# Query tables that read the queries by grid column from a copy made by GpSimd

## The chip, the cores and the metric

The kernel runs on one core of one Trainium2 chip. The metric is the device time of one execution in microseconds (us), from three runs. One further execution was recorded by the hardware profiler; all durations below come from it. The engines are PE (TensorE, with its weight loads shown apart as PEld), DVE (VectorE), ACT (ScalarE), POOL (GpSimd) and SP (which only issues DMAs here).

## The reference

The program is a small audio tower: a token mixer with a linear attention, an expert layer that adds the two best of eight experts, an attention with relative positions in two directions, and a second expert layer with one expert per token. Only the third part matters here. There are B = 4 batches of N = L = 750 tokens, and 12 heads of 64.

```python
def rel_pos_embed(N, table_v, table_h):
    n = N - 1
    s = int(n ** 0.5)                       # 27
    r = jnp.arange(n)
    dv = r[None, :] // s - r[:, None] // s
    dh = r[None, :] % s - r[:, None] % s
    iv = jnp.clip(dv, -L, L) + L + 1        # L = 14
    ih = jnp.clip(dh, -L, L) + L + 1
    iv = jnp.pad(iv, ((1, 0), (1, 0)))
    ih = jnp.pad(ih, ((1, 0), (1, 0)))
    return table_v[iv] + table_h[ih]
...
attn = jnp.einsum('bhid,bhjd->bhij', q, k) * scale
rpk = rel_pos_embed(N, rk_v, rk_h)
attn = attn + jnp.einsum('bhid,ijd->bhij', q, rpk) * scale
attn = jax.nn.softmax(attn, axis=-1)
out = jnp.einsum('bhij,bhjd->bhid', attn, v)
rpv = rel_pos_embed(N, rv_v, rv_h)
out = out + jnp.einsum('bhij,ijd->bhid', attn, rpv)
return out.transpose(0, 2, 1, 3).reshape(B, N, H * HD) @ wproj + bproj
```

All tokens but one stand on a grid of 27 columns: 749 = 27 * 27 + 20, so the grid has 28 rows, of which the last has only 20 tokens. A query's product with the relative embedding depends only on the query's own row (or column) and the key's row (or column). So for each grid row g, the queries of that row are multiplied by one small table, and for each grid column by another.

## The kernel before, in words

**Halves.** The attention goes through 8 halves: 4 batches by 2 groups of 6 heads (HG = 6, held as NPR = 3 pairs of heads, two heads on 128 partitions). A half has a long stretch of 36 steps (`words`: scores, exponentials, products with the values, at about 3 us a step) and ends in a boundary, where the work of two halves meets: `value_tables` finishes the old half, `query_tables` prepares the new one, and `boundary` projects the old output and begins the new maxima. A loop runs over the first 3 batches; the fourth is written out after it. The first half's `query_tables` stands ahead of the loop, so 7 of the 8 lie in a boundary between two halves.

**What holds the queries.** `pairs` is a tile of 128 partitions by 3 by 750 in float32. ACT fills it (L2382) from PE's products of the new half, six pieces of 375 tokens. The last pieces come just after the old half's last step.

**The query tables (L2118 to L2145).** PE makes seven sets of products into four PSUM banks (the `t_banks`, two in tile a_S and two in a_M): sets 0 to 2 are the grid rows (table `rqv`), sets 3 to 5 the grid columns (table `rqh`), set 6 token 749 alone. A matmul of a row reads 27 tokens that lie side by side in each of the three pairs (81 numbers a partition). A matmul of a column reads every 27th token (`pairs[:, :, g:g + GRID * (n - 1) + 1:GRID]`, L1980), 28 or 27 of them in each pair (84 or 81 numbers), 108 bytes apart. A float32 matmul has two records in the trace, and two tables are worked at a time, in the left and the right 64 columns of the array. Sets 0 and 1 have 24 matmuls together, set 2 has 4, sets 3, 4 and 5 have 12, 8 and 7.

**Who empties the banks.** `relative_rows` copies every set to `work`, ACT the even heads (L2427), DVE the odd heads (L2726), both in the order of the sets. Since there are four banks, PE may begin set m only when both have copied set m - 4, and the products of the values (`token_values`, L2176) wait for the fifth and sixth set. When all seven sets are out on both sides, ACT rounds the queries (`qhi`, L2438), and only then can the maxima begin (L2150).

**DVE's order at a boundary** is written by hand: parts of the keys (L2632), the reciprocal of the sums (L2654), the additions of the column part of the values (L2666, paced by PE's L2112), three multiplications by the reciprocals (L2671; these come back through DRAM, issued by SP at L1898), then its part of `relative_rows` (L2726), then the projection's additions and the maxima.

**GpSimd** does one thing in this stage: `qlo`, the rest of the rounded queries, six subtractions of 127x750 a half (L1970). It idles through the boundary until ACT has written `qhi`.

Of the kernel before, what the change touches and what calls it, by code (L numbers as in the profile page):

```python
# [12 lines left out]
F32 = mybir.dt.float32  # L13
# [3 lines left out]
ALU = mybir.AluOpType  # L17
# [3 lines left out]
B, D, L = 4, 64, 750  # L21
KS = (3, 5, 7)
E = len(KS) * D
CH, P = 6, 125
# [729 lines left out]
RING = 4  # L754
# [47 lines left out]
def moe(nc, keep, A, h, ident, cfg, out, st=None, w1=None, wr=None, row=None, room=None, share=None, Y=None,  # L802
# [4 lines left out]
    with ctx:  # L807
# [3 lines left out]
        def sem(n):  # L811
            return keep.enter_context(nc.semaphore(f"{name}_{n}"))
# [9 lines left out]
        n = sb("n", [P, NT, E]) if cfg.gated else None  # L822
# [7 lines left out]
        if not cfg.gated:  # L830
            n = xn
# [18 lines left out]
        if not known:  # L850
            st = sb("st", [P, NT, 6])
# [68 lines left out]
        psY = ctx.enter_context(nc.psum_tensor(f"{name}_psY", [128, 512], F32))  # L920


        s_w, s_r, s_z, s_X, s_cst = sem("w"), sem("r"), sem("z"), sem("X"), sem("cst")

        s_v, s_ln, s_sd, s_n = sem("v"), sem("ln"), sem("sd"), sem("n")
# [8 lines left out]
        s_lt, s_lc = sem("lt"), sem("lc")  # L934
        s_col, s_turn = sem("col"), sem("turn")

        s_in = [sem(f"in{j}") for j in range(RING)]
        s_st = [sem(f"st{j}") for j in range(RING)]

# [782 lines left out]
class Room:  # L1722
# [5 lines left out]
    def __init__(self, nc, sb):  # L1728


        wq, wkv = sb("wq", [128, 4, HG * HD], F32R), sb("wkv", [128, 4, HG * HD], F32R)
        wp = sb("wp", [128, NPR, E])
        rqv, rqh = sb("rqv", [128, NVG + 1, 64]), sb("rqh", [128, GRID + 1, 64])
        rv = sb("rv", [128, NVG + 1, 64])
        bp = sb("bp", [P, E])
        qhi, qlo = sb("qhi", [128, HG, L], F32R), sb("qlo", [128, QLO, L], F32R)
        khi, klo = sb("khi", [128, HG, L], F32R), sb("klo", [128, HG, L], F32R)
        work = sb("work", [128, HG, LW])
        pairs = sb("pairs", [128, NPR, L])
        outs = sb("outs", [128, NPR, LW])  # L1740

        turning = sb("turning", [128, GRID * NVG])

        vhi, vlo = sb("vhi", [P, CH, HG, 128], F32R), sb("vlo", [P, CH, HG, HD], F32R)


        hn = sb("hn", [128, 3, L + 2], F32R)

        PT = sb("PT", [P, 2, 2 * HP])
        Phi, Plo = sb("Phi", [P, 2, 2 * HP], F32R), sb("Plo", [P, 2, 2 * HP], F32R)  # L1750

# [12 lines left out]
        later = [vhi[:].rearrange("p c h d -> p (c h d)").bitcast(F32), vlo[:].rearrange("p c h d -> p (c h d)").bitcast(F32)]  # L1764

        def tokens(x, lo):
            return x[:, lo * CH * E:(lo + 1) * CH * E].rearrange("p (c e) -> p c e", e=E)

        self.got = [[tokens(flat[k], 0) for k in range(2)]] + [[tokens(later[0], 2 * b + k) for k in range(2)]
                                                               for b in range(2)] + [[tokens(later[1], k) for k in range(2)]]  # L1770
        self.all = (wq, wkv, wp, rqv, rqh, rv, bp, qhi, qlo, khi, klo, work, pairs, outs, turning, vhi, vlo, hn, PT, Phi, Plo, nb, rdb, dcol, oh, ohT, st, rstd, mv_, mean, nmx, mrow)


def window_attention(nc, keep, A, h, ident, W4, room, share, Y0, s_back, mv1, rstd1, w11, X1):

    ctx = ExitStack()
    with ctx:
        def sem(n):
            return keep.enter_context(nc.semaphore(f"a1_{n}"))

        (wq, wkv, wp, rqv, rqh, rv, bp, qhi, qlo, khi, klo, work, pairs, outs, turning, vhi, vlo, hn, PT, Phi, Plo, nb, rdb, dcol, oh, ohT, st, rstd, mv_, mean, nmx, mrow) = room.all
        psS = [ctx.enter_context(nc.psum_tensor(f"a1_S{i}", [128, 2, 512], F32)) for i in range(2)]
        psM = ctx.enter_context(nc.psum_tensor("a1_M", [128, 2, 512], F32))
        psO = ctx.enter_context(nc.psum_tensor("a1_O", [128, 2, 512], F32))

        s_bpw = sem("bpw")
        s_bp = sem("bp")
        s_wkv, s_wq, s_wp = sem("wkv"), sem("wq"), sem("wp")  # L1790
        s_w, s_oh, s_oz, s_og = sem("w"), sem("oh"), sem("oz"), sem("og")
# [18 lines left out]
            "table_product": 2 * NTS,  # L1810
            "table_rows_act": 2 * NTS,
            "table_rows_dve": 2 * NTS,
            "qhi_ready": 12,
            "qlo_ready": 12,
            "row_scores": 72,
# [132 lines left out]
        @block.gpsimd  # L1948
        def _(pool):

            for u in range(HG):
                pool.memset(klo[64:128, u].bitcast(F32), 0.0)
            for u in range(QLO):
                pool.memset(qlo[64:128, u].bitcast(F32), 0.0)
            pool.memset(work[0:64, :, L:LW], 0.0)
            pool.memset(turning[64:128], 0.0)
            for u in range(HG):
                last = pool.memset(work[64:128, u], 0.0)
            last.then_inc(s_oz, 1)
            pool.wait_ge(s_oz, 1)  # L1960
            keep.clear_old(pool)
            with pool.Fori(0, B) as i:
                wait = waiter(pool, i)
                for half in range(2):
                    for u in range(half * HG, half * HG + HG):

                        wait("qhi_ready", u + 1)
                        if u % HG >= QLO:
                            wait("scores_ready", (u - QLO + 1) * CH)
                        pool.tensor_tensor(qlo[0:ONE, u % HG % QLO, :], work[0:ONE, u % HG, 0:L],  # L1970
                                           qhi[0:ONE, u % HG, :].bitcast(F32), ALU.subtract
                                           ).then_inc(sg["qlo_ready"], 1)

        def query_tokens(side, g, n):

            if side == "v":
                return pairs[:, :, GRID * g:GRID * g + n]
            return pairs[:, :, g:g + GRID * (n - 1) + 1:GRID]

        def group_tokens(view, side, g, n):  # L1980
# [34 lines left out]
        def _(pe):  # L2015
# [99 lines left out]
                                start=True, stop=True)  # L2115
                    last.then_inc(sg["rel_product"], 1)

            def query_tables(i, half):  # L2118

                wait = waiter(pe, i)  # L2120
                wait("pairs_ready", half * 6 + 6)
# [9 lines left out]
                for m, (side, runs) in enumerate(TABLE_SETS):  # L2131
                    bank_free(m)
                    table = rqv if side == "v" else rqh
                    for a in range(max(len(gs) for gs, n in runs)):
                        for z, (gs, n) in enumerate(runs):
                            if a < len(gs):
                                last = nc.tensor.matmul(
                                    t_banks[m % 4][64 * z:64 * z + 64, a * NPR * n:(a + 1) * NPR * n],
                                    table[:, gs[a] + 1, :], query_tokens(side, gs[a], n), start=True, stop=True)
                    last.then_inc(sg["table_product"], 1)  # L2140
                m = NTS - 1
                bank_free(m)
# [195 lines left out]
            keys_part(0, 0, 5)  # L2338
            pe.wait_ge(s_w, 16 * 3)
            pe.wait_ge(s_oz, 1)  # L2340
            query_tables(0, 0)
            boundary(None, (0, 0))

            pe.wait_ge(s_og, 1)
# [606 lines left out]
```

## Time and profile before

| | |
|---|---|
| three runs, median | 1724.31 us |
| lowest and highest | 1723.38 and 1725.91 us |
| profiled execution, first to last instruction | 1721.1 us |
| PE busy | 1534.4 us (89%), 10815 records |
| DVE busy | 1190.8 us (69%) |
| ACT busy | 988.4 us (57%) |
| POOL busy | 341.2 us (20%), 79.1 us of it `qlo` |
| mean granted TensorE clock | 0.947 of full speed |

The profile gives the execution's span, and no time of its own beyond that; the span stands 3.2 us under the median of the runs. The attention stage runs from about 400 to 1510 us. PE is busy nearly all of it, but a busy PE isn't PE at its peak, and at each boundary it waits several times. What an edit is worth there is read from which engine comes last at each wait, not from these shares. The granted clock of PE has two levels, 1.00 (2.4 GHz) and 0.50 (1.2 GHz).

### The profile page before, as it was taken

Reading aid. Unit: us, or ns where it says so; the run is one execution under the profiler, and the core shown is the slowest. Engines: PE = TensorE matmul, PEld = TensorE weight load, DVE = VectorE, ACT = ScalarE, POOL = GpSimd, SP = SyncE. Lnnn points to the kernel's source line nnn. Section 1 sums busy time; section 2 is a strip of 40 time slices with the busy share of each in tenths; the row PEclk is TensorE's granted clock in tenths of the full one; section 3 lists DMA queues with packets and bytes.
Section 4 is the critical chain, followed back from the end, with each engine's and each line's share of the span. In section 5 each row is a group of like instructions: output and inputs, shape, how many; then the busy total and the mean of one; then the engine's idle time right before and its main releaser. Section 6 shows DMA issues by size and latency. Waiting matters only on the chain. (4 is left out here: it accounts for less than half of the span.)

```text
span 1721.1 us, 32129 instructions
## 1 busy us (share of the span) xinstructions
PE 1534.4 (89%) x10815; PEld 1409.8 (82%) x10816; DVE 1190.8 (69%) x2245; ACT 988.4 (57%) x1777; POOL 341.2 (20%) x499
## 2 busy tenths in 40 slices
PE   5983999937999999899999999999999999848997
PEld 5762999936898898899898899998989889737996
DVE  4887555549775786786787677678677678575443
ACT  5541222226677578578677667667757757562221
POOL 5131566640000000110100010000000010014443
PEclk9985999968999999999999999999999999958999
DMA  8212111164101101100110110110010111091221
GB/s 266 70 51 80 48 57 57 56 142 120 44 11 38 45 11 39 46 11 19 30 44 11 31 45 20 30 44 20 29 45 10 39 35 51 20 291 49 63 58 29
DMA packets 61936, 94.83 MB, mean 55 GB/s; under 512 B 15644, under 2 KB 46511, under 8 KB 61422
## 3 DMA queue, kind: packets, MB, share of 16 engines
q1 hardware_dynamic: 52606, 72.92, 14.7%
q0 software_dynamic: 9200, 20.21, 4.1%
q8 instruction: 78, 1.28, 0.3%
q14 instruction: 52, 0.43, 0.1%
HBM read 72.58 MB, written 21.06 MB: 54 GB/s over the span
## 5 line engine op out<-in xcount | busy, mean ns | idle before, releaser
L2678 DVE TENSOR_REDUCE a_nmx<-a_M 125x1 f32<-125x752 f32 x256 | 240.7, 940 | 129.7 <-PE a_M L2150 128.8
L2500 ACT ACTIVATE a_Phi<-a_S 125x756 fp32r<-125x756 f32 x288 | 231.0, 802 | 156.2 <-PE a_O L2273 146.5
L2803 DVE TENSOR_TENSOR a_Plo<-a_PT,a_Phi 125x756 fp32r<-125x756 f32 x288 | 280.9, 975 | 52.5 <-ACT a_PT L2500 51.7
L1970 POOL TENSOR_TENSOR a_qlo<-a_work,a_qhi 127x750 fp32r<-127x750 f32 x48 | 79.1, 1656 | 996.0 <-PE a_S L2254 509.3
L2500 ACT ACTIVATE a_PT<-a_S 125x756 f32<-125x756 f32 x288 | 230.0, 799 | 0.0
L2254 PE MATMUL a_S<-a_qhi,a_khi 128*125 128x378 f32 x576 | 155.4, 351 | 12.9 <-issue 6.1
L2266 PE MATMUL a_O<-a_Phi,a_vhi 125*128 125x378 f32 x576 | 150.3, 342 | 1.3 <-ACT a_PT L2500 1.3
L2273 PE MATMUL a_O<-a_Plo,a_vhi 125*128 125x378 f32 x576 | 147.5, 337 | 1.0 <-DVE a_Plo L2803 0.9
L2254 PE MATMUL a_S<-a_qhi,a_klo 128*125 128x378 f32 x576 | 146.9, 336 | 0.0
L2254 PE MATMUL a_S<-a_qlo,a_khi 128*125 128x378 f32 x576 | 146.9, 336 | 0.0
L2269 PE MATMUL a_O<-a_Phi,a_vlo 125*64 125x378 f32 x576 | 146.4, 336 | 0.0
L2150 PE MATMUL a_M<-a_khi,a_qhi 127*125 127x376 f32 x512 | 132.2, 339 | 0.4 <-DVE a_nmx L2678 0.4
L1215 PE MATMUL m_psY<-m_w,m_hidT 128*128 x696 | 130.0, 331 | 2.7 <-DVE m_hidT L1572 2.7
L1215 PEld LDWEIGHTS m_psY<-m_w,m_hidT 128*128 128x128 f32 x696 | 114.4, 190 | 9.5 <-issue 9.5
L2254 PEld LDWEIGHTS a_S<-a_qhi,a_khi 128*125 128x125 f32 x576 | 98.3, 187 | 26.4 <-issue 13.5
L2273 PEld LDWEIGHTS a_O<-a_Plo,a_vhi 125*128 125x128 f32 x576 | 104.1, 189 | 14.4 <-DVE a_Plo L2803 4.3
L1299 ACT ACTIVATE m_xT<-m_psX 128x128 fp32r<-128x128 f32 x85 | 23.6, 277 | 155.8 <-PE m_psX L1139 155.8
L1151 PE MATMUL m_psG<-m_w,m_xT 128*128 x540 | 110.9, 352 | 0.5 <-issue 0.4
L2266 PEld LDWEIGHTS a_O<-a_Phi,a_vhi 125*128 125x128 f32 x576 | 102.0, 190 | 11.1 <-issue 8.1
L2254 PEld LDWEIGHTS a_S<-a_qhi,a_klo 128*125 128x125 f32 x576 | 103.9, 187 | 0.0
L2254 PEld LDWEIGHTS a_S<-a_qlo,a_khi 128*125 128x125 f32 x576 | 103.8, 187 | 0.0
L1151 PEld LDWEIGHTS m_psG<-m_w,m_xT 128*128 128x128 f32 x540 | 93.7, 190 | 5.4 <-issue 3.2
(440 smaller groups left out, 3050.3 us busy)
## 6 DMA issues: line engine op xcount, KB each, us to landing
a_qhi<-a_rdens SPq DMA_DIRECT2D x48, 187.5 KB, 3.4
a_wkv<-a_w4k SPq DMA_DIRECT2D x8, 768.0 KB, 5.1
a_wq<-a_w4q SPq DMA_DIRECT2D x8, 768.0 KB, 6.6
a_wkv<-a_w4v SPq DMA_DIRECT2D x8, 768.0 KB, 5.6
m_w<-in_m_w SPq DMA_DIRECT2D x8, 576.0 KB, 9.3
m_X<-m_xn SPq DMA_DIRECT2D x8, 504.0 KB
m_w<-in_m_w SPq DMA_DIRECT2D x8, 384.0 KB, 6.2
m_w_ahead<-in_m_w SPq DMA_DIRECT2D x8, 384.0 KB, 8.1
```

The source lines that it names most:

```text
L1151: last = nc.tensor.matmul(psG[buf][:, g, 0:half], tokens, w1[0:rows_, bass.ds(e, 1), k, g * half:(g + 1) * half].rearrange("d o f -> d (o ...
L1215: last = nc.tensor.matmul(psY[:, 0:E], hidT[:, k * 128:(k + 1) * 128], w2[:, bass.ds(here, 1), k, :].rearrange("f o e -> f (o e)"), start= ...
L1299: nc.scalar.activation(xT[:, buf, 0, :], psX[:, 0:SLOT], ACT.Copy)
L1970: pool.tensor_tensor(qlo[0:ONE, u % HG % QLO, :], work[0:ONE, u % HG, 0:L], qhi[0:ONE, u % HG, :].bitcast(F32), ALU.subtract).then_inc(sg[ ...
L2150: last = nc.tensor.matmul(bank[0:P, a, 0:376], qhi[0:ONE, u % HG, c * P:(c + 1) * P], khi[0:ONE, u % HG, a * 374:a * 374 + 376], start=Tru ...
L2254: last = nc.tensor.matmul(psS[wd % 2][0:P, a, 0:HP], kk[:, u % HG, at], qq[:, PART[a]:PART[a] + HP], start=(x == 0), stop=(x == 2))
L2266: nc.tensor.matmul(psO[:, a, 0:HP], vhi[:, c, u % HG, :], Phi[:, wd % 2, at[a]], start=(c == 0), stop=False)
L2269: nc.tensor.matmul(psO[0:HD, a, 0:HP], vlo[:, c, u % HG, :], Phi[:, wd % 2, at[a]], start=False, stop=False)
L2273: last = nc.tensor.matmul(psO[:, a, 0:HP], vhi[:, c, u % HG, :], Plo[:, wd % 2, at[a]], start=False, stop=(c == CH - 1))
L2500: last = nc.scalar.activation(to[:, wd % 2, :].rearrange("p (a l) -> p a l", a=2), psS[wd % 2][0:P, :, 0:HP], ACT.Exp, scale=SCALE)
L2678: v.tensor_reduce(nmx[:, u % 2, c:c + 1], bank[0:P, :, 0:376], AX.XY, ALU.max, negate=True).then_inc(sg["max_ready"], 1)
L2803: v.tensor_tensor(Plo[:, wd % 2, :], PT[:, wd % 2, :], Phi[:, wd % 2, :].bitcast(F32), ALU.subtract).then_inc(sg["exp_rest"], 1)
```

## The change

GpSimd gets a second job at each of the 7 boundaries between halves. When the old half's last product with the values is done and the new half's queries are all in `pairs`, it copies `pairs` into a new tile `by_column` (128 partitions by 3 by 750), sorted by grid column: 20 columns of 28 tokens, then 7 columns of 27. That takes 9 copies, 3 a pair of heads. The tile lies over the memory of `PT` and the first part of `Phi`, which the old half's last steps have just finished reading, and which the new half writes only after its query tables. Sets 3 to 5 of `query_tables` then read 28 or 27 tokens side by side, and the first matmul of set 3 waits for GpSimd's last copy. The query tables of the very first half read as before. A semaphore `turning` is added that nothing waits for, and a few semaphores of the expert layers are created in another order.

```diff
+        with ExitStack() as early:
+            by_column = early.enter_context(nc.sbuf_tensor("a1_by_column", [128, NPR, L], F32))
         PT = sb("PT", [P, 2, 2 * HP])
...
+            def turn_pairs(i, half):
+
+                wait = waiter(pool, i)
+                wait("values_added", (half + 1) * HG * CH)
+                if half == 0:
+                    wait("pairs_ready", 12)
+                else:
+                    waiter(pool, i + 1)("pairs_ready", 6)
+                pool.sem_inc(s_turning, 1)
+                full = FULL * NVG
+                rows = pairs[:, :, 0:GRID * GRID].rearrange("p h (a b) -> p h b a", b=GRID)
+                last_row = pairs[:, :, GRID * GRID:L - 1].rearrange("p h (b o) -> p h b o", o=1)
+                to = by_column[:, :, 0:full].rearrange("p h (b a) -> p h b a", a=NVG)
+                for pr in range(NPR):
+                    pool.tensor_copy(to[:, pr, :, 0:GRID], rows[:, pr, 0:FULL, :])
+                    pool.tensor_copy(to[:, pr, :, GRID:NVG], last_row[:, pr])
+                    last = pool.tensor_copy(by_column[:, pr, full:L - 1].rearrange("p (b a) -> p b a", a=GRID),
+                                            rows[:, pr, FULL:GRID, :])
+                last.then_inc(sg["pairs_turned"], 1)
...
+            with pool.Fori(0, B - 1) as i:
+                queries_rest(i, 0)
+                turn_pairs(i, 0)
+                queries_rest(i, 1)
+                turn_pairs(i, 1)
+            queries_rest(B - 1, 0)
+            turn_pairs(B - 1, 0)
+            queries_rest(B - 1, 1)
...
-        def query_tokens(side, g, n):
+        def query_tokens(side, g, n, turned):
 
             if side == "v":
                 return pairs[:, :, GRID * g:GRID * g + n]
+            if turned:
+                lo = NVG * min(g, FULL) + (NVG - 1) * max(g - FULL, 0)
+                return by_column[:, :, lo:lo + n]
             return pairs[:, :, g:g + GRID * (n - 1) + 1:GRID]
...
                 for m, (side, runs) in enumerate(TABLE_SETS):
                     bank_free(m)
                     table = rqv if side == "v" else rqh
+                    if m == 3 and turned:
+                        if half == 1:
+                            wait("pairs_turned", 1)
+                        else:
+                            waiter(pe, i - 1)("pairs_turned", 2)
...
-            query_tables(0, 0)
+            query_tables(0, 0, False)
```

On PE, in the loop's first boundary, the end of the row sets and the column sets before (sets 3, 4, 5 and 6; each row is a form of matmul and its count):

```order
L2137 MATMUL a_M<-a_pairs,a_rqv 64x81 x2
L2137 MATMUL a_M<-a_pairs,a_rqh 64x84 x12
L1845 REGISTER_ALU
L2137 MATMUL a_S<-a_pairs,a_rqh 64x84 [waits a1_table_rows_dve,a1_table_rows_act]
L2137 MATMUL a_S<-a_pairs,a_rqh 64x84 x7
L1845 REGISTER_ALU
L2137 MATMUL a_S<-a_pairs,a_rqh 64x81 [waits a1_table_rows_dve,a1_table_rows_act]
L2137 MATMUL a_S<-a_pairs,a_rqh 64x81 x6
```

and the same place in the changed kernel:

```order
L2177 MATMUL a_M<-a_pairs,a_rqv 64x81 x2
L1848 ISA
L2177 MATMUL a_M<-a_by_column,a_rqh 64x84 [waits a1_pairs_turned]
L2177 MATMUL a_M<-a_by_column,a_rqh 64x84 x11
L1848 REGISTER_ALU
L2177 MATMUL a_S<-a_by_column,a_rqh 64x84 [waits a1_table_rows_dve,a1_table_rows_act]
L2177 MATMUL a_S<-a_by_column,a_rqh 64x84 x7
L1848 REGISTER_ALU
L2177 MATMUL a_S<-a_by_column,a_rqh 64x81 [waits a1_table_rows_dve,a1_table_rows_act]
L2177 MATMUL a_S<-a_by_column,a_rqh 64x81 x6
```

No matmul moves: there are as many, in the same order, with the same waits for DVE and ACT, and one wait more, ahead of set 3.

On GpSimd, in the changed kernel's loop, where the first half's last `qlo` is followed by the second half's first (the wait names `s_pair` and `s_rep` are the numbers that `scores_ready` and `values_added` have here):

```order
L1993 TENSOR_TENSOR a_qlo<-a_work,a_qhi 127x750 [waits s_pair]
L1848 REGISTER_ALU
L1848 REGISTER_ALU [waits s_rep]
L1980 COPY a_by_column<-a_pairs 128x20x27 [waits a1_pairs_ready]
L1981 COPY a_by_column<-a_pairs 128x20
L1982 COPY a_by_column<-a_pairs 128x189
L1980 COPY a_by_column<-a_pairs 128x20x27
L1981 COPY a_by_column<-a_pairs 128x20
L1982 COPY a_by_column<-a_pairs 128x189
L1980 COPY a_by_column<-a_pairs 128x20x27
L1981 COPY a_by_column<-a_pairs 128x20
L1982 COPY a_by_column<-a_pairs 128x189
```

Before, the two `qlo` followed each other there; now nine copies stand between them.

## Rows read from the trace of the kernel before

**Rows 1.** PE's forms, whole span: line, names, shapes, count | busy us, mean ns
```profile
L2137 PE MATMUL a_M<-a_pairs,a_rqh 128*64 128x84 f32 x192 | 18.6, 350 | 0.0
```

**Rows 2.** PE's timeline at the third boundary: start us, us, group [idle before]
```profile
819.72 1.91 PE L2137 MATMUL a_S<-a_pairs,a_rqv 128*64 128x81 f32 x48
821.46 0.51 PE L2137 MATMUL a_M<-a_pairs,a_rqv 128*64 128x81 f32 x7
...
821.88 2.14 PE L2137 MATMUL a_M<-a_pairs,a_rqh 128*64 128x84 f32 x23
824.88 2.84 PE L2137 MATMUL a_S<-a_pairs,a_rqh 128*64 128x84 f32 x30 [0.85 <-DVE a_work L2726]
...
829.40 2.08 PE L2176 MATMUL a_S<-a_wkv,a_hn 128*125 128x384 f32 x10 [1.51 <-DVE a_work L2726]
...
844.84 0.65 PE L2254 MATMUL a_S<-a_qhi,a_khi 128*125 128x378 f32 x2
```

**Rows 3.** DVE's timeline at the third boundary
```profile
820.72 2.64 DVE L2671 TENSOR_TENSOR a_outs<-a_outs,a_qhi 128x750 f32<-128x750 f32 x3
823.39 2.72 DVE L2726 COPY a_work<-a_S 29x486 f32<-29x486 f32 x4
826.13 2.06 DVE L2726 COPY a_work<-a_M 29x243 f32<-29x243 f32 x4
828.23 1.99 DVE L2726 COPY a_work<-a_S 28x336 f32<-28x336 f32 x4
```

**Rows 4.** ACT's timeline at the third boundary
```profile
809.33 0.48 ACT L2382 ACTIVATE a_pairs<-a_M 128x375 f32<-128x375 f32 x1 [0.16 <-PE a_M L2032]
...
826.44 1.00 ACT L2427 ACTIVATE a_work<-a_S 28x336 f32<-28x336 f32 x2 [0.92 <-PE a_S L2137]
...
831.01 0.83 ACT L2438 ACTIVATE a_qhi<-a_work 127x750 fp32r<-127x750 f32 x1 [2.01 <-issue]
```

**Rows 5.** GpSimd's forms, whole span
```profile
L1970 POOL TENSOR_TENSOR a_qlo<-a_work,a_qhi 127x750 fp32r<-127x750 f32 x48 | 79.1, 1656 | 996.0 <-PE a_S L2254 509.3 <-ACT a_qhi L2438 486.7
...
L1952 POOL MEMSET a_klo<- 64x750 f32 x6 | 4.0, 719 | 3.8 <-POOLq L807 3.8
...
L1955 POOL MEMSET a_work<- 64x42 f32 x1 | 0.1, 131 | 0.0
```

**Rows 6.** GpSimd's timeline: a `qlo` in a step, and the first two after a boundary
```profile
597.99 1.78 POOL L1970 TENSOR_TENSOR a_qlo<-a_work,a_qhi 127x750 fp32r<-127x750 f32 x1 [14.03 <-PE a_S L2254]
...
556.07 3.28 POOL L1970 TENSOR_TENSOR a_qlo<-a_work,a_qhi 127x750 fp32r<-127x750 f32 x2 [61.26 <-ACT a_qhi L2438]
```

**Rows 7.** DVE's timeline beside those, and one step later
```profile
599.17 1.41 DVE L2803 TENSOR_TENSOR a_Plo<-a_PT,a_Phi 125x756 fp32r<-125x756 f32 x1
...
602.16 0.95 DVE L2803 TENSOR_TENSOR a_Plo<-a_PT,a_Phi 125x756 fp32r<-125x756 f32 x1
...
558.40 0.55 DVE L2694 TENSOR_TENSOR a_vlo<-a_S,a_vhi 125x384 fp32r<-125x384 f32 x1
...
561.30 0.55 DVE L2694 TENSOR_TENSOR a_vlo<-a_S,a_vhi 125x384 fp32r<-125x384 f32 x1
```

**Rows 8.** The reciprocals' way back at the third boundary: SP's issue, and landing in us
```profile
814.76 1.10 SPq L1898 DMA_DIRECT2D a_qhi<-a_rdens  x2
...
a_qhi<-a_rdens SPq DMA_DIRECT2D x2, 187.5 KB, 3.4
```

**Rows 9.** Stretches: length, PE, PEld, DVE, ACT, POOL busy (records), PEclk, DMA, GB/s
```profile
551.60:555.00 3.40, 1.91 (x14) 1.71 (x13) 2.98 (x8) 1.21 (x5) 0.00 (x0) 1.00 0.00 0
555.00:558.40 3.40, 3.40 (x13) 3.40 (x12) 0.27 (x2) 3.02 (x5) 2.33 (x2) 0.50 0.01 2
...
824.70:828.10 3.40, 3.02 (x34) 2.78 (x34) 3.27 (x7) 2.14 (x5) 0.00 (x0) 1.00 0.00 0
```

**Rows 10.** PE's timeline at the first boundary: first query table, first scores of the half
```profile
543.88 1.90 PE L2137 MATMUL a_S<-a_pairs,a_rqv 128*64 128x81 f32 x48
...
570.56 0.65 PE L2254 MATMUL a_S<-a_qhi,a_khi 128*125 128x378 f32 x2
```

More of the change, by code:

```diff
@@ L920, in moe @@
         psY = ctx.enter_context(nc.psum_tensor(f"{name}_psY", [128, 512], F32))
+        s_in = [sem(f"in{j}") for j in range(RING)]
+        s_st = [sem(f"st{j}") for j in range(RING)]
         s_w, s_r, s_z, s_X, s_cst = sem("w"), sem("r"), sem("z"), sem("X"), sem("cst")
@@ L935, in moe @@
         s_col, s_turn = sem("col"), sem("turn")
-        s_in = [sem(f"in{j}") for j in range(RING)]
-        s_st = [sem(f"st{j}") for j in range(RING)]
         s_w1 = {} if cfg.gated else {e: sem(f"w1_{e}") for e in range(LOADED, NE)}
@@ L1770, in __init__ @@
                                                                for b in range(2)] + [[tokens(later[1], k) for k in range(2)]]
-        self.all = (wq, wkv, wp, rqv, rqh, rv, bp, qhi, qlo, khi, klo, work, pairs, outs, turning, vhi, vlo, hn, PT, Phi, Plo, nb, rdb, dcol, oh, ohT, st, rstd, mv_, mean, nmx, mrow)
+        self.all = (wq, wkv, wp, rqv, rqh, rv, bp, qhi, qlo, khi, klo, work, pairs, outs, turning, vhi, vlo, hn, PT, Phi, Plo, nb, rdb, dcol, oh, ohT, st, rstd, mv_, mean, nmx, mrow, by_column)
 def window_attention(nc, keep, A, h, ident, W4, room, share, Y0, s_back, mv1, rstd1, w11, X1):
@@ L1779, in sem @@
             return keep.enter_context(nc.semaphore(f"a1_{n}"))
-        (wq, wkv, wp, rqv, rqh, rv, bp, qhi, qlo, khi, klo, work, pairs, outs, turning, vhi, vlo, hn, PT, Phi, Plo, nb, rdb, dcol, oh, ohT, st, rstd, mv_, mean, nmx, mrow) = room.all
+        (wq, wkv, wp, rqv, rqh, rv, bp, qhi, qlo, khi, klo, work, pairs, outs, turning, vhi, vlo, hn, PT, Phi, Plo, nb, rdb, dcol, oh, ohT, st, rstd, mv_, mean, nmx, mrow, by_column) = room.all
         psS = [ctx.enter_context(nc.psum_tensor(f"a1_S{i}", [128, 2, 512], F32)) for i in range(2)]
@@ L1784, in window_attention @@
         psO = ctx.enter_context(nc.psum_tensor("a1_O", [128, 2, 512], F32))
-        s_bpw = sem("bpw")
+        s_bpw, s_turning = sem("bpw"), sem("turning")
         s_bp = sem("bp")
@@ L1812, in window_attention @@
             "table_rows_dve": 2 * NTS,
+            "pairs_turned": 2,
             "qhi_ready": 12,
@@ L1961, in _ @@
             keep.clear_old(pool)
-            with pool.Fori(0, B) as i:
+            def turn_pairs(i, half):
                 wait = waiter(pool, i)
[L1964 to L1972, printed above, removed]
@@ new lines, in queries_rest @@
+            def queries_rest(i, half):
+                wait = waiter(pool, i)
+                for u in range(half * HG, half * HG + HG):
+                    wait("qhi_ready", u + 1)
+                    if u % HG >= QLO:
+                        wait("scores_ready", (u - QLO + 1) * CH)
+                    pool.tensor_tensor(qlo[0:ONE, u % HG % QLO, :], work[0:ONE, u % HG, 0:L],
+                                       qhi[0:ONE, u % HG, :].bitcast(F32), ALU.subtract
+                                       ).then_inc(sg["qlo_ready"], 1)
@@ L2116, in value_tables, with query_tables @@
                     last.then_inc(sg["rel_product"], 1)
-            def query_tables(i, half):
+            def query_tables(i, half, turned=True):
                 wait = waiter(pe, i)
@@ L2138, in query_tables @@
                                     t_banks[m % 4][64 * z:64 * z + 64, a * NPR * n:(a + 1) * NPR * n],
-                                    table[:, gs[a] + 1, :], query_tokens(side, gs[a], n), start=True, stop=True)
+                                    table[:, gs[a] + 1, :], query_tokens(side, gs[a], n, turned), start=True, stop=True)
                     last.then_inc(sg["table_product"], 1)
```

## The prediction

> **What bounds the kernel now.** The totals say that PE is busy 89% of the span, so the first view to open is PE's list of groups with the shapes kept apart: the column sets have 192 records in bank tile a_M, 24 a half [rows 1]. So there are 8 such places, and 7 of them are changed. The second view is PE's timeline at one of them; I take the third boundary, where the clock stays at full speed [rows 2]. There the 48 records of the row sets 0 and 1 start within 821.46 - 819.72 = 1.74 us, 36 ns a record. The records of column set 3 take 81 ns each: 23 of them last 2.14 us, of which the last one's own 350 ns [rows 1] comes off, (2.14 - 0.35) / 22. Those of sets 4 and 5 take (2.84 - 0.35) / 29 = 86 ns. Reading every 27th number thus costs more than twice as much as reading 81 side by side, and the change is aimed at something real.
>
> The third view tells what that is worth: DVE's timeline at the same boundary [rows 3]. From 820.72 to 830.22 us DVE has no gap over 0.05 us: three multiplications to 823.36, the copies of sets 0 and 1 to 826.11, of sets 2 and 3 to 828.19, of sets 4 and 5 to 830.22, with set 6 behind them. It never waits for PE there. PE waits for it instead: 0.85 us ahead of set 4, until DVE has set 0 out (half of the first 2.72 us, 824.75), and 1.51 us ahead of the values' products at 829.40, until DVE has set 4 out (half of the 1.99 us, 829.23) [rows 2, 3]. ACT, the other emptier, does wait for PE, 0.92 us ahead of set 4, but it ends at 831.01 - 2.01 = 829.00, and then stands 2.01 us until DVE is done [rows 4]. So the boundary is bound by DVE, and the column matmuls lie in its shadow.
>
> **The change part by part.** *Faster column sets.* At 36 ns a record, set 3 would save 24 x 45 = 1.1 us and sets 4 and 5 would save 30 x 50 = 1.5 us, 2.6 us a boundary and 18 us over 7. Now place them. Set 3 ends 1.1 us sooner, and set 4 still starts at 824.88, since its wait is for DVE's copy of set 0; the 1.1 us become idle time. Set 4's 16 records then take 0.6 us, but set 5 waits for DVE's copy of set 1, at 826.11. Set 5 takes 0.5 us, and set 6 waits for DVE's copy of set 2, in the group that starts at 826.13. DVE reaches set 3 in the second half of that group, set 4 at 828.23 and set 5 about 1 us later. Even before the change each was ready by then. ACT ends about 1 us sooner and waits 3 us for DVE in place of 2. The values' products start at 829.40 as before. Both ends for this term: 0, and -18 us if PE were what ends last. I take 0, since the rows show PE waiting for DVE both ahead of set 4 and after set 6.
>
> *The copies.* No row shows GpSimd copying float32 with a stride. Each pair moves 540 + 20 + 189 = 749 numbers in 3 instructions. Below, by the fill of 750 numbers at 719 ns and of 42 at 131 ns [rows 5]: 0.72 + 2 x 0.12 = about 1.0 us a pair, 2.9 us in all. Above, by `qlo`, which reads two inputs of 750 at 1656 ns [rows 5]: 1.66 + 0.24 = 1.9 us a pair, 5.7 us. If the stride slows it as it does PE (86 / 36 = 2.4 times) it is 13.6 us. I take 5.7, as `qlo` is the nearest row that reads. They can start when ACT has written the last queries, 809.33 + 0.48 = 809.81 [rows 4], and are wanted at 821.75, 11.9 us later. At 5.7 us they end 6 us early. At 13.6 us set 3 would start 1.7 us late and still end (24 x 36 ns = 0.9 us) at 824.4, ahead of 824.88. So the new wait costs nothing on PE below some 14 us. Behind the last copy on GpSimd stands `qlo`, which waits for `qhi` at 831 anyway. The Trainium skill's "GPSIMD Engine Reference", section "Performance pitfalls for Q7 kernels", gives about 2.9 cycles an element for reads whose step exceeds 8 bytes; by the 1.2 GHz of its specifications that is an estimate of 5.4 us plus the starts. No row here tests it, and the sum would be the same.
>
> *DVE beside the copies.* A `qlo` that ran from 597.99 to 599.77 stretched the DVE subtraction that began at 599.17 to 1.41 us, against 0.95 in the next step; a subtraction with one input in PSUM took 0.55 us with `qlo` running and 0.55 without [rows 6, 7]. This agrees with the Trainium skill's "SBUF — State Buffer", "SBUF: two separate sides", by which GpSimd and a DVE instruction with two SBUF inputs exclude each other. Between 810 and 816 DVE's work reads PSUM as one input, apart from one reciprocal on 75x20, of SBUF alone. If it is held for one copy, about 1.2 us (540 of 749 of 1.66), the way back of the sums slips as much: the two DMAs are issued within 814.76 to 815.86 and land 3.4 us later, by 819.3, and are wanted at 820.72 [rows 3, 8]. That leaves 1.4 us. At the boundaries between batches the reciprocal comes before the copies. Term: 0, at most a few tenths.
>
> *The clock.* This is where idle time of PE can cost something. At the first boundary PE was busy 1.91 of the 3.40 us from 551.60 on, waiting for DVE, and then ran at 0.50, the 1.2 GHz level, from 555.00 to 558.40 [rows 9]. From the first query table to the half's first scores it took 570.56 - 543.88 = 26.68 us there, and 844.84 - 819.72 = 25.12 us at the third [rows 2, 10]. One such fall costs 1.56 us. The change takes 1.5 us of PE's busy time out of the stretch 824.70 to 828.10, where it had 3.02 [rows 9]: that leaves about 1.5, less than the 1.91 after which the clock fell. The first boundary has paid the price already, the third has not; if no other has, up to 6 more can, 9.4 us. Whether the slow reads count as activity at all is not shown. The two boundaries had the same work and the same waits, and one had the fall, so it depends on how a boundary happens to lie in time. I take 1 or 2 more, 2 us.
>
> **The sum.** 0 + 0 + 0 + 2 us on a profiled span of 1721.1; the runs' median stands 3.2 us above it, so 1724.3 + 2 = 1726.3 us.
>
> **The rivals.**
> *Clock falls at most boundaries.* Slower. Place: the products of values and the projection after 829.40, which PE bounds. For it: the emptied stretch above. Against it: the same columns are streamed in the same stretch, only sooner in it. With 4 to 6 more falls, 6.2 to 9.4 us: 1730.5 to 1733.7. From 3 falls on it counts as slower.
> *PE comes last after all.* Faster. If the column sets' time came through whole it would be 1724.3 - 18 = 1706 us; if a third of it did, because ACT's earlier end or the earlier bank counts, 1718. For it: ACT waits 0.92 us for PE, and the maxima after the boundary are PE's and DVE's in turn. Against it: DVE's 9.5 us without a gap.
> *GpSimd holds DVE.* Slower. If the reciprocal loses to all nine copies in a row, it ends 5.7 us late; less the 1.4 us of slack that is 4.3 us at each of the 4 boundaries within a batch, 17 us, 1741. Against it: `qlo` held DVE once and for its own length only.
> *The change doesn't speed the reads*: then nothing moves, 1724.
>
> **How the numbers follow.** A difference under 0.2% (3.4 us) can't be told from none. The forecast, DVE still sets the pace with 0 to 2 more falls of the clock: 0.50, 1724 to 1728. No quicker reads: 0.02. Clock at most boundaries: 0.36. PE last, whole or in part: 0.09. GpSimd holds DVE: 0.03. Faster by over 0.2% is then 0.09, within 0.2% 0.52, slower 0.39. The likeliest case gives 1726.3. The range reaches up over the clock's case to 1733, and down to 1721.5, a fall less and a little gained by ACT; what is left out is the gain in full and the held DVE.
>
> **What would show it.** In the changed profile the records of the column sets should stand 35 to 40 ns apart in place of 81 to 86; PE's idle ahead of set 4 should grow from 0.85 to about 2 us, with DVE named; DVE's copies should follow the multiplications without a gap, and PE's values' products should start 9.7 us after the first query table, as before. The copies should end before set 2, some 4 to 6 us after the last queries. The granted clock late in each boundary tells the price: count the stretches at 0.50. It would be wrong if those products started sooner after the first query table than 9.5 us, or if set 3 named POOL as what it waited for.

## The result, and the profile after

The changed kernel took 1733.55 us (1733.23 to 1735.44, 4 runs), the kernel before 1723.85 us beside it (1722.51 to 1725.91). The ratio is 1.0059, interval 1.0046 to 1.0071: slower by about 10 us. (One execution of the kernel before, beside the later experiments on another chip, took 7569.11 us at the full clock; it is left out of every ratio.) The forecast of 1726.3 us was wrong, and the time lies just above the range, where the rival "Clock falls at most boundaries" had put it. The profiled execution went from a span of 1721.1 to 1731.4 us.

**The page.** Busy times of the changed kernel, and the clock granted to PE in 40 slices:

```profile
PE 1535.4 (89%) x10815; PEld 1411.6 (82%) x10816; DVE 1191.0 (69%) x2245; ACT 988.1 (57%) x1777; POOL 380.2 (22%) x562
PEclk9995999968999999999999999999999999867999
```

PE's share is 89% as before. Slices of 43 us are too wide to show stretches of 3 to 7 us at the low clock, so the boundaries have to be opened one by one.

**PE at a boundary.** The seventh boundary is the best one to read: its start ran at the full clock before and after. PE's timeline in the changed kernel (start us, us, group, idle before):

```profile
1370.09 1.91 PE L2177 MATMUL a_S<-a_pairs,a_rqv 128*64 128x81 f32 x48
...
1372.24 1.04 PE L2177 MATMUL a_M<-a_by_column,a_rqh 128*64 128x84 f32 x23
1375.14 0.80 PE L2177 MATMUL a_S<-a_by_column,a_rqh 128*64 128x84 f32 x16 [1.86 <-DVE a_work L2766]
1376.51 0.74 PE L2177 MATMUL a_S<-a_by_column,a_rqh 128*64 128x81 f32 x14 [0.57 <-DVE a_work L2766]
...
1379.66 3.53 PE L2216 MATMUL a_S<-a_wkv,a_hn 128*125 128x384 f32 x10 [2.11 <-DVE a_work L2766]
```

Set 3's 23 records last 1.04 us where they lasted 2.14 [rows 2], so the reads are as quick as row sets. The time saved has all become idle time of PE: 1.86 us ahead of set 4 (0.85 before, [rows 2]), 0.57 ahead of set 5 (none before) and 2.11 ahead of the values' products (1.51 before). Those products start 1379.66 - 1370.09 = 9.57 us after the first query table. In the kernel before they did so 9.59 us after it at this boundary, and 9.68 at the third. But the ten products then last 3.53 us, against 2.08 [rows 2]: they run at the low clock.

**DVE at the same boundary**, to be read against [rows 3]:

```profile
1370.98 2.64 DVE L2711 TENSOR_TENSOR a_outs<-a_outs,a_qhi 128x750 f32<-128x750 f32 x3
1373.65 2.71 DVE L2766 COPY a_work<-a_S 29x486 f32<-29x486 f32 x4
1376.39 2.06 DVE L2766 COPY a_work<-a_M 29x243 f32<-29x243 f32 x4
1378.48 1.99 DVE L2766 COPY a_work<-a_S 28x336 f32<-28x336 f32 x4
```

No gap, and the same durations. DVE sets the pace as before.

**GpSimd's copies**, its forms over the whole span:

```profile
L1980 POOL COPY a_by_column<-a_pairs 128x540 f32<-128x540 f32 x21 | 26.3, 1250 | 286.6 <-ACT a_pairs L2422 286.6
```

The big copies take 1250 ns. The nine copies of the third boundary start at 809.29 and end at 814.28 + 0.54 = 814.82:

```profile
809.29 1.27 POOL L1980 COPY a_by_column<-a_pairs 128x540 f32<-128x540 f32 x1 [39.36 <-ACT a_pairs L2422]
...
811.12 1.25 POOL L1980 COPY a_by_column<-a_pairs 128x540 f32<-128x540 f32 x1
...
814.28 0.54 POOL L1982 COPY a_by_column<-a_pairs 128x189 f32<-128x189 f32 x1
```

That is 5.5 us, and it is over 4.7 us before the half's first query table (819.57). The Trainium skill's "GPSIMD Engine Reference", section "Performance pitfalls for Q7 kernels", with its 2.9 cycles an element, gives an estimate of 1.3 us for 540 numbers; the trace agrees with 1.25.

**The boundaries, one row each.** Stretches of the changed kernel from the values' products to the first scores of the new half (length, busy us and records of PE, PEld, DVE, ACT, POOL, then PEclk, DMA, GB/s):

```profile
551.60:568.55 16.95, 16.01 (x83) 15.36 (x84) 12.02 (x23) 7.14 (x12) 3.28 (x2) 0.90 0.01 3
690.84:709.49 18.65, 16.37 (x83) 15.30 (x84) 12.90 (x25) 7.14 (x12) 3.29 (x2) 0.91 0.01 3
829.11:845.73 16.62, 15.69 (x83) 15.06 (x84) 12.02 (x23) 7.14 (x12) 3.28 (x2) 0.91 0.01 2
967.99:986.94 18.95, 16.31 (x84) 15.33 (x84) 12.91 (x25) 7.14 (x12) 3.28 (x2) 0.91 0.01 3
1106.67:1122.12 15.45, 14.51 (x84) 13.73 (x84) 12.03 (x23) 7.15 (x12) 3.29 (x2) 1.00 0.01 2
1244.42:1261.29 16.87, 15.94 (x83) 15.26 (x84) 12.02 (x23) 7.14 (x12) 3.29 (x2) 0.90 0.01 1
1379.66:1397.45 17.79, 16.84 (x84) 16.23 (x84) 12.02 (x23) 7.25 (x12) 3.29 (x2) 0.85 0.00 1
sum 121.28, PE 111.68 PEld 106.28 DVE 85.91 ACT 50.11 POOL 23.00; mean PE 15.95 PEld 15.18 DVE 12.27 ACT 7.16 POOL 3.29
```

The same in the kernel before, the first and the last two of its seven and the sum:

```profile
553.56:570.56 17.00, 16.07 (x84) 15.29 (x84) 12.02 (x23) 7.13 (x12) 3.28 (x2) 0.90 0.01 2
...
1241.77:1257.12 15.35, 14.42 (x83) 13.65 (x84) 12.02 (x23) 7.76 (x15) 3.29 (x2) 1.00 0.01 1
1375.52:1390.96 15.44, 14.48 (x84) 13.71 (x84) 12.02 (x23) 7.14 (x12) 3.28 (x2) 1.00 0.01 1
sum 113.60, PE 103.57 PEld 97.53 DVE 85.91 ACT 50.90 POOL 23.00; mean PE 14.80 PEld 13.93 DVE 12.27 ACT 7.27 POOL 3.29
```

Read the clock column: six of seven now hold a stretch at the low clock, where one did before. The sums say 7.7 us, and PE's busy time alone rises by 8.1 us with the same number of records.

What PE did ahead of such a fall is seen in shorter stretches. The changed kernel's seventh boundary:

```profile
1374.80:1378.20 3.40, 1.84 (x34) 1.58 (x34) 3.27 (x7) 2.93 (x6) 0.00 (x0) 1.00 0.00 0
1378.20:1381.60 3.40, 1.94 (x6) 1.97 (x7) 2.49 (x7) 1.02 (x3) 0.00 (x0) 0.50 0.00 0
1381.60:1385.00 3.40, 3.40 (x12) 3.40 (x12) 0.00 (x0) 2.44 (x5) 3.18 (x2) 0.50 0.00 0
```

And the kernel before, where the same 34 records stand:

```profile
1370.60:1374.00 3.40, 3.01 (x34) 2.79 (x34) 3.27 (x7) 2.24 (x5) 0.00 (x0) 1.00 0.00 0
1374.00:1377.40 3.40, 1.89 (x11) 1.77 (x11) 2.55 (x7) 1.70 (x5) 0.00 (x0) 1.00 0.00 0
```

The 34 records of sets 4 to 6 took 3.01 us of PE's time and take 1.84 now. (The stretch of 3.4 us that begins 4.7 us after the first query table was busy for 2.9 to 3.4 us at all seven boundaries before, and for 1.8 to 2.8 us after.) Behind them the clock goes to 0.50, the 1.2 GHz level, and stays there for 6.8 us, into the work that PE bounds. The kernel before had an equally empty stretch right after (1.89), and no fall here: what a stretch of this kind leads to can't be told from its busy time alone.

**The account of the profiled spans, +10.3 us.** Up to the first query table of the first changed boundary -2.0 us (541.92 against 543.88 [rows 10]); nothing is changed there, and the executions recorded for this study put that point anywhere from 541.9 to 546.1. In the seven boundaries +8.5: +7.7 in the rows above, +1.0 between them, in value tables (two falls of 6.8 us begin in these, one before), -0.2 from query tables to values' products. And +3.8 after the last boundary, where the last half's value tables run at the low clock:

```profile
1490.80:1497.60 6.80, 6.79 (x100) 6.77 (x102) 0.44 (x2) 1.73 (x3) 0.00 (x0) 0.50 0.04 5
```

In the kernel before that clock fell later, when PE had little to do:

```profile
1493.70:1500.50 6.80, 3.23 (x10) 3.25 (x11) 5.74 (x9) 0.32 (x1) 0.00 (x0) 0.50 0.00 0
```

### The profile page after: what moved, and what is told of

Read it like the earlier page. It is cut to its first block and busy times, and to the rows that moved or that the text cites. A ratio compares the mean times of both kernels' runs of the same rounds, so it can differ in the third digit from the quotient of the medians.

```text
span 1731.4 us, 32200 instructions
## 1 busy us (share of the span) xinstructions
PE 1535.4 (89%) x10815; PEld 1411.6 (82%) x10816; DVE 1191.0 (69%) x2245; ACT 988.1 (57%) x1777; POOL 380.2 (22%) x562
```

## The experiments

Below, T is the start of the values' products and S that of the first scores; "T to S" is the stretch of the tables above, and its sum over the seven boundaries was 113.6 us before and 121.3 after. A late fall is a stretch at 0.50 that begins at or after 2 us ahead of T and before S. An early fall is one that begins about the first query table, from 3 us ahead of it to 1 us behind it; the kernel before has three in its profile, the changed kernel six in its first. Each time is told against the kernel before on the same chip.

### Copies kept, reads as before

```diff
-    table[:, gs[a] + 1, :], query_tokens(side, gs[a], n, turned), start=True, stop=True)
+    table[:, gs[a] + 1, :], query_tokens(side, gs[a], n, False), start=True, stop=True)
```

> The changed kernel with GpSimd's nine copies, the new wait and the new order of semaphores kept, but with the column matmuls reading every 27th query from pairs, as before. The theory (the quick reads empty PE's part of the boundary, and the granted clock falls more often): this is the kernel before in all that matters, 1722 to 1726 us, column records 81 to 86 ns apart, granted clock at 0.50 late in a boundary at no more than 2 of the 7. The rival (the copies, the wait or the semaphores cost the time): 1731 to 1735 us.

Measured: 1726.33 us against 1725.74, ratio 1.0005 (0.9995 to 1.0016). Its sum T to S:

```profile
sum 111.49, PE 101.74 PEld 95.74 DVE 85.92 ACT 52.14 POOL 23.03; mean PE 14.53 PEld 13.68 DVE 12.27 ACT 7.45 POOL 3.29
```

No late fall. The 9 copies, the wait ahead of set 3, the new tile and the semaphores cost nothing that can be measured: by the interval, at most 0.16%, 2.8 us. The sum T to S isn't the whole price of the clock, though. It is 2.1 us under the kernel before, and the time is the same, since from S to the next first query table the six stretches are 3.4 us longer in sum (669.4 against 666.0 us), with six early falls in place of three.

### Quick reads, no copies

Sets 3 to 5 read runs of neighbouring tokens of `pairs`, which are the wrong tokens; nothing is copied and nothing waited for.

```diff
-    return by_column[:, :, lo:lo + n]
+    return pairs[:, :, lo:lo + n]
```

> The changed kernel without GpSimd's copies and without the wait for them; the column matmuls read 28 or 27 numbers side by side straight from pairs, which are the wrong tokens. The theory (quick reads alone bring the clock down): 1730 to 1735 us, with the clock at 0.50 late in at least 5 of the 7 boundaries. The rival (the copies cost the time): 1721 to 1726 us.

Measured: 1737.25 against 1725.74, ratio 1.0063 (1.0050 to 1.0076). Two of its seven stretches, and the sum:

```profile
695.69:715.32 19.63, 16.99 (x83) 16.07 (x84) 12.91 (x25) 7.25 (x12) 3.28 (x2) 0.87 0.01 3
...
1248.75:1266.40 17.65, 16.72 (x83) 16.07 (x84) 12.02 (x23) 7.25 (x12) 3.29 (x2) 0.86 0.00 1
...
sum 122.23, PE 112.65 PEld 107.20 DVE 85.92 ACT 50.42 POOL 22.98; mean PE 16.09 PEld 15.31 DVE 12.27 ACT 7.20 POOL 3.28
```

The whole loss comes with the quick reads alone (it is 2 us above the range foreseen). Five boundaries have late falls, four of them 6.8 us long. These cost more than the 1.56 us taken: 17.65 against 15.35 is 2.3, 19.63 against 17.51 is 2.1.

### The quick sets twice

Each matmul of sets 3 to 5 is issued twice, at the same bank and with the same operands, so PE has about its old amount of work again, read quickly.

```diff
-    for a in range(max(len(gs) for gs, n in runs)):
+    for a in list(range(max(len(gs) for gs, n in runs))) * (2 if m >= 3 and turned else 1):
```

> The changed kernel, but PE works the matmuls of the column sets 3, 4 and 5 twice each before it hands the set over (54 more records a boundary at 36 ns, 1.9 us more PE work at each of 7 boundaries, all of it where PE would wait for DVE). The theory: with about the PE activity of before in that stretch the clock stays up, so that more work is quicker: 1720 to 1727 us. The rival (the loss has nothing to do with how busy PE is there, but with the shift in time or with the copies): 1731 to 1737 us.

Measured: 1727.63 against 1725.74, ratio 1.0011 (1.0000 to 1.0021). Its sum T to S:

```profile
sum 114.79, PE 103.49 PEld 97.47 DVE 85.93 ACT 52.25 POOL 23.02; mean PE 14.78 PEld 13.92 DVE 12.28 ACT 7.46 POOL 3.29
```

There are 54 records more a boundary, and nearly all of the loss is gone. One late fall is left, at the first boundary, where the kernel before had it too. The 1.2 us by which the sum stands above 113.6 are at the second boundary at the full clock, where PE idles 3.02 us ahead of S in place of 1.79, and the profile names nothing that it waited for.

### The kernel before with half of the column matmuls

Of the 27 column products of sets 3 to 5 only 14 are issued (6 of 12, 4 of 8, 4 of 7), 28 records in place of 54 a boundary; the rest of those tables is left out. The reads are the slow ones, and there are no copies.

```diff
-    for a in range(max(len(gs) for gs, n in runs)):
+    for a in range(0, max(len(gs) for gs, n in runs), 2 if m >= 3 and (i is not 0 or half) else 1):
```

> The kernel before, strided reads and all, but every second matmul of the column sets is left out at the 7 boundaries (14 of 27 are made; the rest of the output of these sets is stale). The theory: less PE work makes it slower, since the stretch is as empty as after the change: 1727 to 1735 us. The rivals: 1722 to 1726 us if DVE alone counts, or less if PE's column work were on the path (4.5 us a boundary halved, 7 x 2.2 = 15 us: 1709).

Measured: 1744.59 against 1725.74, ratio 1.0103 (1.0088 to 1.0119). PE's timeline at its sixth boundary, and its sum T to S:

```profile
1250.08 0.86 PE L2137 MATMUL a_S<-a_pairs,a_rqh 128*64 128x84 f32 x8 [1.84 <-DVE a_work L2726]
1251.45 0.84 PE L2137 MATMUL a_S<-a_pairs,a_rqh 128*64 128x81 f32 x8 [0.52 <-DVE a_work L2726]
...
1254.61 3.53 PE L2176 MATMUL a_S<-a_wkv,a_hn 128*125 128x384 f32 x10 [2.11 <-DVE a_work L2726]
```
```profile
sum 129.23, PE 119.74 PEld 114.69 DVE 85.92 ACT 50.76 POOL 22.99; mean PE 17.11 PEld 16.39 DVE 12.27 ACT 7.25 POOL 3.28
```

The idle times are those of the changed kernel (1.84, 0.52 and 2.11, against 1.86, 0.57 and 2.11), made by leaving work out rather than by quicker reads. All seven boundaries now have a late fall of 6.8 us, 15.6 us in the sum. The kernel that issues less work is 19 us slower, 10 us above the range foreseen. So it is the emptiness that costs, not the copy, the new tile or the kind of read. That it costs more here than with the change was not expected: the idle times are the same, but all seven boundaries fall in place of five or six, and all for 6.8 us. Why is open.

### Filling the gap ahead of set 6

Two kernels: the one with the quick sets twice, and the kernel before, each with 24 matmuls more between set 5 and set 6, which write columns of set 6's bank that nothing reads. (In the second, the matmuls read `pairs` directly.)

```diff
+    for g in range(12 if turned else 0):
+        for z in range(2):
+            nc.tensor.matmul(t_banks[m % 4][64 * z:64 * z + 64, 8:8 + NPR * NVG], rqh[:, g + 1, :],
+                             query_tokens("h", g, NVG, turned), start=True, stop=True)
```

> As the last experiment with the column sets worked twice, and PE makes 24 more matmuls of 84 columns (48 records, 1.7 us) ahead of set 6, into columns of that bank that nobody reads: they fill the 2 us in which PE would wait for DVE's set 4. The theory (the clock follows how busy PE is in these stretches): hardly a late fall, at most 1 or 2 of 7, and 1719 to 1725 us, at or below the kernel before, with about 102 records a boundary that compute nothing. The rival (PE's work there doesn't decide; set 3 to 5 twice helped for another reason): 1727 to 1735 us, since 1.7 us of work are added.

> The kernel before, strided reads and no copies, with the same 24 filler matmuls ahead of set 6. The theory: the kernel before pays for late falls too, in some of its boundaries, so 1719 to 1724 us, 1 to 5 under the kernel before. The rival (before has no such cost): 1724 to 1730 us, the filler's 1.7 us standing in part in the way of the values' products.

Measured: 1728.56 against 1726.85, ratio 1.0008 (0.9996 to 1.0021), and 1728.52, ratio 1.0010 (0.9998 to 1.0023). Both times hoped for were missed. The late falls did go in both. The sum T to S of the first:

```profile
sum 111.59, PE 101.58 PEld 96.32 DVE 83.90 ACT 52.33 POOL 23.01; mean PE 14.51 PEld 13.76 DVE 11.99 ACT 7.47 POOL 3.29
```

But the filler itself came last where the clock had fallen already, about the first query table. The second kernel at its third boundary:

```profile
820.70 3.51 PE L2137 MATMUL a_S<-a_pairs,a_rqv 128*64 128x81 f32 x48
...
829.43 1.95 PE L2145 MATMUL a_M<-a_pairs,a_rqh 128*64 128x84 f32 x46
...
831.49 0.79 PE L2180 MATMUL a_S<-a_wkv,a_hn 128*125 128x384 f32 x3
```

The row sets take 3.51 us in place of 1.91, the filler ends at 831.4, and T comes 10.79 us after the first query table in place of 9.7. What the clock gave back was spent on holding it. The kernel before had one late fall to lose, so it had little to gain.

### ACT takes set 4 from DVE

If DVE's nine microseconds without a gap set the pace, a set less for DVE must move T. On the changed kernel, and later on the kernel before, ACT copies set 4's odd heads too; the counts that the waits of PE and ACT look for are adapted. (`odd` is the bank's upper part of 32 partitions.)

```diff
+    if par and m == 4:
+        continue
...
+    if m == 4:
+        last = copy(grid_columns(work[at:at + rows, 1::2, :], 0, gs, n),
+                    odd.rearrange("p (g h n) -> p h n g", h=NPR, n=n))
...
-    wait("table_rows_dve", half * NTS + 5 + c)
+    wait("table_rows_dve", half * (NTS - 1) + (1 if c == 0 else 5))
```

> The changed kernel, but ACT copies both halves of set 4 and DVE none of it, so that the values' products no longer wait for DVE's fifth set. The theory (DVE is what ends last, the quick reads are in its shadow): PE's values' products start about 8 us after the first query table in place of 9.7, and 7 x 1.5 = 10 us go: 1721 to 1727 us, clock falls kept. The rival (the boundary is bound by PE or by the way back of the sums): no change against the changed kernel, 1732 to 1736 us.

> The kernel before with ACT copying both halves of set 4, strided reads and no copies by GpSimd. ACT then waits for PE's set 4, which comes about 1 us later than with quick reads. The theory (DVE's fifth set sets the start of the values' products; the slow reads keep the clock up): products start about 8.9 us after the first query table, 7 x 0.7 = 5 us gained with few late falls, 1719 to 1723 us, about as good as the same edit on the changed kernel. The rival (the quick reads are worth something once DVE isn't last, clock or no clock): 1723 to 1727 us, clearly above that kernel.

Measured, on the changed kernel: 1719.51 against 1726.85, ratio 0.9958 (0.9941 to 0.9974). On the kernel before: 1720.89 against 1726.29, ratio 0.9971 (0.9955 to 0.9988). Both beat the kernel before, and with it the changed one; the first is 1.5 us under its range, the second within it. PE's timeline of the first, third boundary:

```profile
817.04 1.91 PE L2183 MATMUL a_S<-a_pairs,a_rqv 128*64 128x81 f32 x48
...
825.07 1.14 PE L2222 MATMUL a_S<-a_wkv,a_hn 128*125 128x384 f32 x5 [0.46 <-ACT a_work L2473]
826.61 1.11 PE L2222 MATMUL a_S<-a_wkv,a_hn 128*125 128x384 f32 x5 [0.40 <-DVE a_work L2772]
...
841.10 0.65 PE L2300 MATMUL a_S<-a_qhi,a_khi 128*125 128x378 f32 x2
```

And of the second, sixth boundary:

```profile
1229.03 1.91 PE L2143 MATMUL a_S<-a_pairs,a_rqv 128*64 128x81 f32 x48
...
1237.80 2.06 PE L2182 MATMUL a_S<-a_wkv,a_hn 128*125 128x384 f32 x10 [0.60 <-ACT a_work L2433]
...
1253.15 0.65 PE L2260 MATMUL a_S<-a_qhi,a_khi 128*125 128x378 f32 x2
```

Where the clock is full, T comes 8.0 us after the first query table with the quick reads, 8.8 without, and 9.5 to 9.7 in the two kernels of the case. But S comes 841.10 - 817.04 = 24.06 us after it with the quick reads and 1253.15 - 1229.03 = 24.12 without, against 25.12 in the kernel before. So ACT's help is worth 1.0 us a boundary with either kind of read, and the 0.7 us by which the quick reads bring T forward are all but gone at the boundary's end: with them the second five products wait 0.40 us for DVE, and the projection starts only 0.15 us sooner (10.52 us after the first query table against 10.67). The two times differ by less than their intervals. The one with quick reads has three late falls in its profile, the other none.

### Both at once, and a smaller filler

ACT takes set 4, and the quick sets twice with the filler; then ACT takes set 4 and only set 3 is issued twice.

```diff
-    for a in range(max(len(gs) for gs, n in runs)):
+    for a in list(range(max(len(gs) for gs, n in runs))) * (2 if m == 3 and turned else 1):
```

> The two together: ACT copies both halves of set 4, the column sets are worked twice and the filler stands ahead of set 6. The theory: if the filler keeps the clock and ends before the values' products may start, both gains add up: 1710 to 1719 us. The rival: now PE is late itself, by 1.0 to 1.9 us of filler a boundary, and it comes out like the filler alone, 1719 to 1726 us.

> The changed kernel with ACT copying both halves of set 4, and column set 3 alone worked twice (24 more records, 0.9 us, where PE would wait for DVE's first set). The theory (falls come from empty stretches, and this filler costs nothing): fewer late falls, 1714 to 1719 us. The rival: no fewer falls, 1718 to 1722 us.

Measured: 1726.94 against 1726.85, ratio 0.9999 (0.9987 to 1.0012), and 1727.21 against 1726.29, ratio 1.0011 (0.9992 to 1.0030). Both gave ACT's gain back. In the first, T comes 9.6 to 10.8 us after the first query table, since PE's own work comes last there. The second at its second boundary:

```profile
681.51 3.04 PE L2183 MATMUL a_S<-a_pairs,a_rqv 128*64 128x81 f32 x48
...
685.08 2.06 PE L2183 MATMUL a_M<-a_by_column,a_rqh 128*64 128x84 f32 x46
...
690.60 1.72 PE L2222 MATMUL a_S<-a_wkv,a_hn 128*125 128x384 f32 x8 [1.52 <-ACT a_work L2473]
```

With the row sets at the low clock, the doubled set 3 ends at about 687.1, T comes 9.09 us after the first query table, and at two other boundaries a late fall comes all the same. Neither theory's time held, nor did the second rival's; the first rival's held within 1 us. Its 12 runs spread from 1719.3 to 1738.6 us, the widest of the study but for the one execution told of above.

### The changed kernel once more

> The changed kernel as it is, on the same chip as the two others, for comparison. Both theories: 1731 to 1738 us.

Measured: 1737.22 against 1726.29, ratio 1.0062 (1.0046 to 1.0077). One of its late falls, 6.8 us long:

```profile
1245.70:1252.50 6.80, 5.08 (x16) 5.11 (x17) 2.76 (x7) 3.70 (x8) 2.85 (x2) 0.50 0.00 0
```

Late falls at five of seven boundaries, four of them of this length; in the first profile it was six of seven, one of this length. The number of falls repeats, the boundaries that have them do not.

Yet there is an order in them. The changed kernel's two profiles and that of the quick reads without copies have 21 boundaries. Nine have no early fall, and each has a late one of 6.8 us. Six have an early fall of 3.4 us, and each has a late one of 3.4 us. Six have an early fall of 6.8 us, and five of these have no late one. An early fall slows the row sets (the 48 records last 3.51 us at the changed kernel's third boundary, 1.91 at its seventh), so that PE is busier between first query table and T: the stretch that begins 4.7 us after the first query table holds 1.84 us of PE's work with no early fall, 2.0 with one of 3.4 us, 2.3 and 2.8 with one of 6.8 us. That this is the reason was not tested.

## Why the prediction was wrong

**The step that failed.** Under "The clock": "I take 1 or 2 more, 2 us." There were 5 more late falls in the profile, four of 3.4 us and one of 6.8, which together cost 7.7 us, 1.54 each, beside 1.56 foreseen. So the mean price held and the count was wrong. That the mean comes out so close is in part luck: the four short ones cost 1.1 to 1.5 us, the long one 2.35. The stretch that the step named did empty much as it said (1.84 us left, about 1.5 foreseen), and it named 1.91 before the one known fall. The count came from the kernel before, where one boundary in seven had the fall and two with the same work and waits differed. But at all of these the slow reads kept PE busy for 2.9 us or more of that stretch, so they say nothing on how many fall when it is at 1.8. "It depends on how a boundary happens to lie in time" was right for the kernel before and was carried over to another one without a reason: of the changed kernel's 14 boundaries in two profiles 11 have a late fall. The half work shows it from the other side: with the same idle times made in another way, all seven fall.

**What the step left out.** A fall can be 6.8 us long, and then costs about 1.9 to 2.8 us: 2.35 at the changed kernel's seventh boundary (17.79 against 15.44), 1.9 to 2.5 at four boundaries of its second profile, up to 2.8 in the half work. And the last half pays 3.8 us in its value tables, a place that the prediction did not look at. The five profiles that have a low stretch of 6.8 us beginning 93.3 to 93.7 us after the last boundary's S (both of the changed kernel, the quick reads without copies, the half work, ACT with set 3 twice) end 334.0 to 334.1 us after S. Six with one of 3.4 us at 94 to 96 us end 331.3 to 332.5 us after it, and two with none there (the kernel before, and it with ACT's help) 330.2 and 330.4. All five of the first kind have a late fall at the seventh boundary, and of the other eight only one has. By what it would be carried over those 90 us is open. With the late falls alone the time would have been 1724.3 + 7.7 = 1732.0 us, inside the range; the last half's 3.8 us, less the 2.0 us at the start that are scatter, brought it out.

**What held.** *Faster column sets*: 36 ns a record, worth nothing on the path, since DVE sets the pace; PE's idle ahead of set 4 grew to 1.86 us, about 2 foreseen, and T stayed 9.5 to 9.7 us after the first query table at all seven; ACT ended 0.7 us sooner at the seventh, where 1 was foreseen. *The copies*: 5.5 us against 5.7, ended before they are wanted, and the first experiment puts copies and wait at 0.6 us, which its interval doesn't tell from none. *DVE beside the copies*: the reciprocal took 0.26 us at 811.75, in the middle of a copy that ran from 811.12, and 0.26 before; it was not held.

**The rivals.** *Clock falls at most boundaries* is what happened, and its 1730.5 to 1733.7 us holds the time measured. The mechanism is its own; that the time falls inside is partly luck, as it has no term for the last half, and beside it the changed kernel stood 10.9 us above the kernel before on another chip (1737.22 against 1726.29), where 6.2 to 9.4 were foreseen. *PE comes last after all* is refuted for this kernel. With DVE relieved, the same quick reads bring T 0.7 us forward but S by under 0.1 us (24.06 against 24.12), so there too they are not worth a time. *GpSimd holds DVE* and *the change doesn't speed the reads* are refuted by the traces.

**What stays open.** Whether slow reads keep the clock by the time they fill or by something of their own: the quick sets twice restore the time and the clock together, so they don't tell the two apart. And why a boundary falls or not: late falls go with the length of the early one, as told above, but what places the early ones is not known, and an equally empty stretch (1.89 us) led to none in the kernel before. Early falls come in every kernel here, and no kernel was tried that removes them.

## What to carry to other kernels

- Where another engine sets the pace, PE's slow reads may be what keeps its clock up: before making work of PE quicker that nothing waits for, look at how busy PE is in the stretch ahead of the next work that PE bounds, and count every such place as one that will pay, not the one that pays already.
- Take work from the engine without a gap first (here one set of copies from DVE to ACT, 5 to 7 us), and only then make the waiting engine quicker; filler on PE keeps the clock but becomes the bound as soon as the clock has fallen before it.

## What was unexpected of the hardware

- PE with less work made the kernel slower: half of the column matmuls left out cost 19 us (1744.59 against 1725.74).
- A stretch at the low clock can lie wholly in dense work: from 1490.80 on PE is busy 6.79 of 6.80 us, at 0.50. Ahead of it, from 1487.40 to 1490.80, PE was busy 1.99 of 3.40 us: the end of the half's steps, and a gap of 1.26 us ahead of the value tables. The kernel before had the same at this place (1.98 of 3.40 us from 1480.91 on) and no fall behind it. PE's timeline of the changed kernel there:

```profile
1488.95 0.61 PE L2313 MATMUL a_O<-a_Plo,a_vhi 125*128 125x378 f32 x2 [0.17 <-DVE a_Plo L2843]
1490.81 0.38 PE L2122 MATMUL a_O<-a_work,a_rv 96*64 96x3 f32 x4 [1.26 <-DVE a_work L2821]
```
